# Attention on one Trainium2 core: key tiles multiplied with the values in pairs, and the row maxima transposed by VectorE

## What is computed

```python
h = _ln(x) * (1.0 + scale_msa) + shift_msa
q = (h @ Wq + bq).reshape(B, L, H, DH)      # B = 2, L = 2048, H = 16, DH = 32
k = (h @ Wk + bk).reshape(B, L, H, DH)
v = (h @ Wv + bv).reshape(B, L, H, DH)
scores = jnp.einsum('blhe,bshe->bhls', q, k)
A = jax.nn.softmax(scale * scores, axis=-1)
out = jnp.einsum('bhls,bshd->blhd', A, v)
```

## Time and profile before

| | before |
|---|---|
| median of three runs | 2636.14 us (2632.66 to 2636.88) |
| span of the profiled execution | 2625.2 us |
| PE (TensorE matmul) busy | 2543.3 us, 97% |
| PEld (TensorE weight load) busy | 1482.7 us, 56% |
| DVE (VectorE) busy | 1841.4 us, 70% |
| ACT (ScalarE) busy | 1309.9 us, 50% |
| POOL (GpSimd) busy | 1625.0 us, 62% |

### The profile page before, as it was taken

How to read it: one execution, slowest core, us unless ns; L and a number is a source line. 1 busy time by engine, 2 the same in 40 slices (tenths; PEclk the granted TensorE clock), 3 DMA queues, 4 the chain that set the end, 5 groups by cost and what they waited for, 6 DMA issues and landing times.

```text
span 2625.2 us, 45742 instructions
## 1 busy us (share of the span) xinstructions
PE 2543.3 (97%) x13208; PEld 1482.7 (56%) x13208; DVE 1841.4 (70%) x2872; ACT 1309.9 (50%) x2429; POOL 1625.0 (62%) x744
## 2 busy tenths in 40 slices
PE   7999899999999999999999999999999979999998
PEld 5788654444444444444444444444444437888887
DVE  5444588887877878778777787778778745555553
ACT  3333245665666656666666665666656642222221
POOL 0000157887888878888878888878888772112120
PEclk9999999999999999999999999999999989999999
DMA  7655631111211112211122111122111001121100
GB/s 263 207 192 167 153 112 49 33 34 39 60 34 33 33 38 56 40 33 33 35 44 56 33 33 35 35 52 46 33 34 33 21 25 53 49 73 71 48 32 32
DMA packets 141459, 163.15 MB, mean 62 GB/s; under 512 B 76048, under 2 KB 92944, under 8 KB 134032
## 3 DMA queue, kind: packets, MB, share of 16 engines
q1 hardware_dynamic: 140480, 159.95, 23.2%
q10 hardware_dynamic: 720, 0.02, 0.0%
HBM read 100.95 MB, written 58.72 MB: 61 GB/s over the span
## 4 chain that ended last, share of the span: by engine, by line
PE 93%; DVE 3%; issue 1%; ACT 1%; DMA 1%; SPq 0%; POOL 0%; ACTq 0%; POOLq 0%; DVEq 0%
PE ps L1113 21%; PE ps L1015 20%; PE ps L1104 19%; PE ps L1127 18%; PE ps L1118 7%; PE ps L1248 7%; DVE part_max L868 1%; PE ps L1024 1%; DVE weights_r L882 1%; PE ps L1059 1%; PE ps L1047 0%; DMA work<-v_rows 0%; DVE work L942 0%; ACT work L670 0%; DMA work<-in_x 0%
## 5 line engine op out<-in xcount | busy, mean ns | idle before, releaser
L538 POOL TENSOR_TENSOR work<-work 128x1024 f32<-128x1024 f32 x640 | 1505.7, 2395 | 296.7 <-PE ps L1118 262.7
L868 DVE TENSOR_REDUCE part_max<-ps 128x1 f32<-128x512 f32 x1984 | 1229.0, 682 | 321.3 <-PE ps L1104 320.7
L670 ACT ACTIVATE work<-ps 128x512 f32<-128x512 f32 x2048 | 1070.9, 602 | 697.3 <-PE ps L1113 697.2
L1113 PE MATMUL ps<-acts_r 97*128 97x512 f32 x2048 | 836.4, 418 | 26.0 <-ACT work L670 14.7
L1104 PE MATMUL ps<-acts_r 96*128 96x512 f32 x1984 | 811.3, 409 | 6.8 <-DVE part_max L868 6.7
L1113 PEld LDWEIGHTS ps<-acts_r 97*128 97x128 f32 x2048 | 383.1, 190 | 396.7 <-ACT work L670 308.4
L1127 PE MATMUL ps<-work 128*32 128x512 f32 x4096 | 545.3, 604 | 0.0
L1104 PEld LDWEIGHTS ps<-acts_r 96*128 96x128 f32 x1984 | 375.6, 189 | 263.0 <-DVE part_max L868 182.4
L1015 PE MATMUL ps<-acts_r,weights_r 128*128 128x512 f32 x1536 | 380.3, 397 | 5.7 <-DVE acts_r L790 5.7
L1015 PEld LDWEIGHTS ps<-acts_r,weights_r 128*128 128x128 f32 x1536 | 291.1, 191 | 69.3 <-issue 6.8
L547 POOL TENSOR_TENSOR work<-work,gate_b 128x512 f32<-128x512 f32 x60 | 84.5, 1439 | 214.3 <-DMA work<-in_x 172.8
(11 more groups left out here) (69 smaller groups left out, 897.5 us busy)
## 6 DMA issues: line engine op xcount, KB each, us to landing
work<-in_x SPq DMA_DIRECT2D x16, 1024.0 KB, 5.4
acts_r<-q_hi SPq DMA_DIRECT2D x64, 256.0 KB, 4.8
acts_r<-k_hi SPq DMA_DIRECT2D x64, 256.0 KB, 6.4
q_hi<-work SPq DMA_DIRECT2D x32, 256.0 KB, 2.6
q_lo<-work SPq DMA_DIRECT2D x32, 256.0 KB, 3.3
k_hi<-work SPq DMA_DIRECT2D x32, 256.0 KB, 2.6
k_lo<-work SPq DMA_DIRECT2D x32, 256.0 KB, 3.2
v_rows<-work SPq DMA_DIRECT2D x32, 256.0 KB, 2.0
```

The source lines that it names most:

```text
L538: nc.gpsimd.tensor_tensor(psum_acc[:, at], first, prob[:, t % RING, at], ALU.add).then_inc(add_ok, 1)
L670: nc.scalar.activation(prob[:, t % RING, j * CH:(j + 1) * CH], ps[:, A_BANKS + (u + t * NQ + j) % B_BANKS, :], ACT.Exp, scale=SCALE).then_ ...
L868: nc.vector.tensor_reduce(part_max[:, f // NQ, f % NQ:f % NQ + 1], ps[:, (u + f) % A_BANKS, :], AX.X, ALU.max).then_inc(a_max, 1)
L1113: nc.tensor.matmul(ps[:, A_BANKS + (u + t * NQ + j) % B_BANKS, :], ks[u][0:M_ROW + 1, t * P:(t + 1) * P], qs[u][0:M_ROW + 1, j * CH:(j + 1 ...
```

## The change

Values and sums are taken only in steps 1, 3, 5, ... 15. Step 1 takes values and sum of tile 15 of the head before and finishes its denominators; step 3 takes tiles 0, 1 and 2; each later odd step t takes tiles t-2 and t-1, with their sums where they are TensorE's. GpSimd adds tile 13 in place of tile 11, so that TensorE's tiles are 4, 8, 11, 14 and 15. The number of groups stays 22. FILLS_AT and SPREAD stay as they are.

VectorE transposes the maxima itself, in four blocks of 32x32, right behind row_maxima. Nothing is negated any more: the row of ones in k becomes a row of minus ones. As each block of 32 queries lies on partitions of its own after that, SyncE puts the row with four DMAs of 16 pieces of 128 bytes. ScalarE copies output and denominators one behind the other, both behind step 1. Two slots of the ring change their roles in the passage to stage 3, with which the first norm there waits for tile 14 in place of tile 13.

```diff
-POOL_TILES = [0, 1, 2, 3, 5, 6, 7, 9, 10, 11, 12]
+POOL_TILES = [0, 1, 2, 3, 5, 6, 7, 9, 10, 12, 13]
+BREAKS = {3: (0, 1, 2), **{t: (t - 2, t - 1) for t in range(5, NT, 2)}}
+STEP_LAST = 1
+MAX_PIECES = 4
-        SLOT_XC1, SLOT_XN3, SLOT_OTF, SLOT_HTF3 = range(RING)
+        SLOT_XC1, SLOT_OTF, SLOT_XN3, SLOT_HTF3 = range(RING)
-        row_max = sb("row_max", [P, NT])
-        neg_max = sb("neg_max", [NT, P], F32R)
+        row_max = sb("row_max", [P, DH])
+        max_T = sb("max_T", [P, DH])
...
-                sp.wait_ge(neg_ok, g + 1)
-                sp.dma_start(qs[u][M_ROW:M_ROW + 1, :].bitcast(F32),
-                             neg_max[:].bitcast(F32)).then_inc(neg_in, 16)
+                sp.wait_ge(maxT_ok, g + 1)
+                row = qs[u][M_ROW:M_ROW + 1, :].bitcast(F32).rearrange("o (t q) -> o t q", q=P)
+                for w in range(MAX_PIECES):
+                    sp.dma_start(row[:, :, w * DH:(w + 1) * DH], max_T[w * DH:w * DH + NT, :]).then_inc(maxT_in, 16)
...
-                    if prev and t == 0:
+                    if prev and t == STEP_LAST:
                         take_output(g - 1, (u + 2) % NBUF, uses)
-                    if prev and t == 1:
                         take_denominator(g - 1)
...
-                nc.vector.tensor_scalar(neg_max[:], ps[0:NT, 0, 0:P], -1.0, None, ALU.mult).then_inc(neg_ok, 1)
+            def transpose_max(g):
+                dve.wait_ge(max_ok, g + 1)
+                if not isinstance(g, int) or g:
+                    dve.wait_ge(maxT_in, g * (16 * MAX_PIECES))
+                nc.vector.transpose(max_T[:], row_max[:]).then_inc(maxT_ok, 1)
...
-            def transpose_max(g):
-                pe.wait_ge(max_ok, g + 1)
-                nc.tensor.matmul(ps[0:NT, 0, 0:P], row_max[:], ident[:], start=True, stop=True).then_inc(maxT_mm, 1)
...
-            def last_values(g, u):
-                values(g, u, NT - 1)
-                if NT - 1 in PE_TILES:
-                    tile_sum(g, NT - 1)
+            def use_tile(g, u, t):
+                values(g, u, t)
+                if t in PE_TILES:
+                    tile_sum(g, t)
...
-                    if t == 0 and prev:
-                        last_values(g - 1, (u + 2) % NBUF)
-                    if t == 1 and prev:
+                    if t == STEP_LAST and prev:
+                        use_tile(g - 1, (u + 2) % NBUF, NT - 1)
                         finish_denominators(g - 1)
-                    if t >= 2 and t - 2 in PE_TILES:
-                        tile_sum(g, t - 2)
-                    if t >= 1:
-                        values(g, u, t - 1)
+                    for tile in BREAKS.get(t, ()):
+                        use_tile(g, u, tile)
                     fill(t, 2)
...
-                    if nxt and t == STEP_MAX:
-                        transpose_max(g + 1)
                 assert next(fills, None) is None
-                if NT - 2 in PE_TILES:
-                    tile_sum(g, NT - 2)
```

## The result

| | before | changed |
|---|---|---|
| median of four runs | 2635.78 us (2632.66 to 2636.88) | 2720.15 us (2719.08 to 2723.01) |
| span of the profiled execution | 2625.2 us | 2721.2 us |
| PE busy | 2543.3 us, 97% | 2598.7 us, 95% |

The ratio is 1.0331 with a 95% interval of 1.0314 to 1.0347: the change makes the kernel 3.3% slower. The forecast was 2719.

What follows compares the result with a forecast made beforehand. TensorE was taken to bound the heads. Its 51.7 us plus stalls make 57.3 against 55.1: +66 us for 30 heads, +13 turns, +3 head 0, +1.5 norm, together +83.5; span 2708.7 plus 10.9 gives 2719, range 2680 to 2758.

Steps and rivals of the forecast that it cites:

- TensorE's work alone: TensorE's starts, entries, exits and groups in a head with eight visits, without waits: 51.7 us, saving 3.4 us a head.
- ScalarE's share: Scores waiting for exponentials: +0.95 us between the visits of steps 1 and 3, +0.59 us between steps 13 and 15.
- The stalls, interval by interval: Waits between visits, added to each head: 0.95 + 1.50 + 0.78 + 0.88 + 0.59 + 0.89 us.
- 15 to 1: From step 15 into the next head: the last fill before the next visit waits for VectorE's reductions, +0.89 us.
- The row: Four DMAs at the head's start land level with VectorE: no cost yet, every 0.1 us more costs 0.1 us a head.
- Rival B: The row's four DMAs land after 3.1 us, making each head 1.3 us longer: 2758 us; chance 0.13, or a part of it.
- The sum for plain heads: TensorE's work plus stalls: a head of 57.3 us against 55.1, +2.2 us, for 30 heads +66 us.
- The turns: At each turn of the loop VectorE's late start now lies on the path: about +1.35 us for ten turns, +13.
- Head 0 and the end: Head 0, with twelve more VectorE operations: +3 us (0 to 8); stage 3's first norm waiting for tile 14: +1.5 (0 to 2).
- What lay around the span: The 10.9 us by which the median of the runs lies above the profiled span, added to 2708.7 to give 2719.
- Rival A: Three banks are enough, no stalls come, and TensorE's 3.4 us for 30 heads is gained: 2534 us; chance 0.05.
- part 2: Long visits leave VectorE idle with three banks; late reductions and exponentials then delay fills and scores by 0.39 to 0.95 us.

## Why the prediction came out right, and where it was only lucky

**TensorE's work alone, 51.7 us a head.** Right. Visits of three groups take 2.71 to 2.73 us and those of two 1.86. The changed kernel with half reductions has heads of 53.16 us, which is 51.7 with ScalarE's share (0.95 + 0.59 forecast) left in it.

**The stalls, interval by interval.** From the end of one visit to the start of the next, in the head of 1254.45:

| interval | forecast | measured |
|---|---|---|
| 1 to 3 | 5.14 | 5.02 |
| 3 to 5, 5 to 7 | 4.94 | 4.94, 4.94 |
| 7 to 9, 11 to 13 | 4.34 | 4.33, 4.33 |
| 9 to 11 | 5.30 | 5.29 |
| 13 to 15 | 3.60 | 3.58 |
| 15 to 1 | 4.61 | 4.86 |

The formulas from the earlier trace rows hold to 0.02 us but for two intervals. In the first, the sixth score starts 3.38 us behind the visit (1264.28, forecast 3.39) and the last fill 4.70 us (forecast 4.71); only the entry into the visit was wrong, 0.32 us and not the 0.43 of a fill that has itself waited. For the last, SP and DVE at the start of that head:

```profile
1250.82 2.42 SPq L395 DMA_DIRECT2D acts_r<-max_T  x4
...
1254.13 0.69 DVE L884 TENSOR_TENSOR work<-work,bv_rows 128x512 f32<-128x512 f32 x1
1255.22 4.28 DVE L875 TENSOR_REDUCE part_max<-ps 128x1 f32<-128x512 f32 x7 [0.40 <-PE ps L1105]
```

The first reduction waits 0.40 us for its fill, and not for the multiplication that ended at 1254.82. The fill stands behind the first score, and the score behind the row. So the row decides there and not VectorE.

**The row.** The transposition takes 0.21 us, and lies within my 0.3 (it writes 128x32 elements, twice as many as L818 and not, as the prediction has it, as many). The landing is nearly as forecast, 1.7 us where I took 1.8:

```profile
DMA to landing us min/median/max: 1.6/1.7/3.0
```

The step of the working that was off is "0.49 to 0.54 from one to the next": four DMAs of 16 pieces of 128 bytes take 2.42 us to issue, so 0.62 us each, where L398's were 0.5. The fourth is issued 1.83 us behind the first and not 1.5. Of these 0.33 us 0.24 came back: the first issue stood 0.11 us earlier than forecast and the landing took 0.13 less. So the row is there 5.54 us behind the last fill (1248.78 to 1254.32), where I had 5.45. The first score starts 0.14 us behind the landing, in all plain heads alike, and for that the prediction had nothing; VectorE, put level with the row, was free 0.16 us earlier than forecast. Together the first reduction comes 6.44 us behind the last fill and not 6.2, which is the 0.25 us above. "Every 0.1 us more costs 0.1 us a head" held, here and in the runs with eight DMAs and with two turns. Rival B's effect is there, at a fifth of its 1.3 us, and not from a slow landing. (The profile puts the wait of this score down to ScalarE in most heads, whose exponential is the other thing it waits for; the time of the landing and the run with eight DMAs show that it is the row.)

**The sum for plain heads.** 57.3 forecast, 57.32 measured; 30 times the difference to 55.1 is +66. That it is right to 0.02 us is luck in part: +0.25 in one interval stands against -0.12 in another and small amounts in the visits.

**The turns.** "About +1.35 for each of ten turns, +13" was too small by half (the rows named there give 2.40 - 0.06 - 0.88 = 1.46, and there are nine such turns and not ten). A turn costs 56.4 - 55.13 = 1.3 us before and 61.2 - 57.3 = 3.9 after, so +2.6 for each of nine, +23. I had priced VectorE's 2.40 us against TensorE's 0.88 and stopped there. Two things came on top. The row is late at a turn as well (at the turn of 956.67 SP takes 3.40 us for its four DMAs), and after the waits the clock falls at some turns. PE at two turns, the second with the spacing of starts behind it:

```profile
961.52 0.50 PE L1114 MATMUL ps<-acts_r 97*128 97x512 f32 x1 [1.60 <-DMA acts_r<-max_T]
963.75 0.50 PE L1105 MATMUL ps<-acts_r 96*128 96x512 f32 x1 [0.56 <-DVE part_max L875]
```
```profile
784.01 0.49 PE L1114 MATMUL ps<-acts_r 97*128 97x512 f32 x1 [1.10 <-ACT work L673]
...
787.33 0.80 PE L1105 MATMUL ps<-acts_r 96*128 96x512 f32 x1 [1.66 <-DVE part_max L875]
787.92 0.63 PE L1114 MATMUL ps<-acts_r 97*128 97x512 f32 x1
788.35 0.63 PE L1105 MATMUL ps<-acts_r 96*128 96x512 f32 x1
...
794.88 0.50 PE L1105 MATMUL ps<-acts_r 96*128 96x512 f32 x1
```

At the second one TensorE waits twice, 1.10 and 1.66 us, the clock falls to its 1.2 GHz level and starts are 0.43 us apart until 794.88. Five of the nine turns are of this kind, with heads of 61.9 to 62.7 us and a clock of 0.80 in the windows shown; the other four keep the clock and take 59.7 to 59.95. SP takes 3.17 to 3.41 us for its four DMAs at the four turns that keep the clock, and 2.76 to 3.12 at the other five, where VectorE's first reduction then makes TensorE wait longer. What decides between the two kinds isn't shown.

**Head 0 and the end.** I put +3 and +1.5. Against the second profile of before, head 0 is 0.6 us shorter (78.6 and 79.2), and the rest of the span 1.7 us shorter. Against the first profile head 0 is 8.8 us longer, at the far end of the bounds I gave; read alone, that would look like an effect of the change. The two profiles of the kernel before differ by as much, so no effect on head 0 can be told from them.

**What lay around the span.** The 10.9 us that I added are not time around the span. They are mostly that the profiled execution had a short head 0. With the second profile as base the sum reads: plain heads +66, turns +23, head 0 -0.6, the rest -2, together +86, from 2635.2 to 2721.2. Mine was +83.5 from a base that stood for the same median (2625.2 + 83.5 + 10.9 are 2719.6, which I gave as 2719). So the 1 us between forecast and result is smaller than the errors in it: turns 10 us too cheap, head 0 and the end 7 us too dear, and over thirty heads the interval 15 to 1 7.5 us too short and that from 1 to 3 3.6 us too long.

**The rivals.** Rival A (enough banks, 2534) fell: even with halved reductions the kernel is at 2603. The prediction's point from which it decides, 3 x 0.60 us of work against the visit, is only half of the condition. With halved reductions three take 1.3 us at most (0.44 each), the visit of 2.73 outlasts them by more than before, and the waits are gone all the same. The other half is that reductions are slower than fills come (0.60 against 0.47 us); it stands in the formulas of part 2, which reckon with 0.60 for each fill, and not in the sentence on the rival.

## What to carry to other kernels

When two producers share TensorE with a burst of other work, ask two things. Does the burst outlast what the banks hold, 3 x 0.60 us here? And does the consumer catch up behind it, that is, is it faster for one tile than the tiles come? Here a burst of 1.0 us was nearly free (0.2 us a head), and one of 2.7 emptied a consumer that needs 0.60 us for what comes every 0.47. By the prediction's sum the merging saves 3.4 us a head and costs 5.6, some 4.2 of it at VectorE and the rest at ScalarE. With a consumer that keeps up, the same idle time costs nothing. Look what an instruction hides before you count it as saved: the transposition's matmul hid ScalarE, and a small visit at the seam hid the loop's turn. And profile the kernel before twice when the sum is to be good to a third of a per cent: the span shown was 9 us too short for the median it was set against.

## What the runs showed of the hardware

- A turn of the hardware loop costs each engine by itself: VectorE's first reduction comes 2.3 to 3.2 us late, and TensorE's first score 0.9 to 1.6 us in the kernel before and 1.8 to 2.5 with the visit in front of it gone. Eight turns less are 11.6 us in the kernel before.
- After one wait of 3.5 us (eight DMAs), or two of 1.1 and 1.7 us close together (a turn of the changed kernel), TensorE was at its 1.2 GHz level, with starts 0.43 us apart; after waits of 1.6, 0.56 and 0.60 us in one head it stayed at 2.4. The length of the wait alone doesn't tell: in the kernel before, 1.56 us at one turn were followed by the lower level (clock 0.79 from 1592 to 1600 us) and 1.58 at another were not (1.00 from 593 to 601).
- SP needs 0.62 us for one of the four DMAs of 16 pieces, up to 0.87 in some heads, and 0.68 for one of the eight with half as many pieces: cutting a row into more DMAs saves nothing on the queue.
- A subtraction of 128x512 on VectorE took 0.68 us or 5.78 us in the same head; the long ones end 0.55 us behind the end of an addition on GpSimd that was under way.
- VectorE transposes 128x32 in blocks of 32x32 in 0.21 us.
- VectorE starts a reduction of 128x512 from PSUM every 0.60 us at best; nine of 128x256 took 3.93 us.
